# Three more pieces of a one-hot pick on ScalarE, and the expert products moved ahead of the gather

## The reference

```python
xn = batch_norm(x)                                # over all 1792 tokens
q = (xn @ w_q.T) ...                              # two halves, 8 heads
sim = einsum('pbnhd,hkpd->pbnhk', q, keys_p)      # 2 x 8 x 32 scores per token
scores, idx = top_k(sim, 8)
sc, pk = top_k(scores[0][..., :, None] + scores[1][..., None, :], 8)   # 8 of 64 pairs
indices = idx0 * 32 + idx1                        # 8 heads x 8 experts per token, of 1024
hmid = sigmoid(sc) * gelu(inputs . down[indices])
out = sum over the 64 of hmid * up[indices]
```

## Time and profile before

| | |
|---|---|
| median of 3 runs | 521.06 us (520.82 to 522.73) |
| the profiled execution | 520.97 us |
| its span, first to last instruction | 519.2 us |
| VectorE busy | 386.6 us, 74% of the span |
| TensorE busy | 442.1 us, 85% |
| ScalarE busy | 219.1 us, 42% |
| GpSimd busy | 141.5 us, 27% |
| the chain that ended last, by engine | PE 43%, DVE 43%, issue 7%, ACT 3%, DMA 1%, POOL 1% |
| its costliest VectorE lines | L880 7%, L945 6%, L884 4%, L911 3% |

### The profile page before, as it was taken

The page is one execution under the profiler, slowest core; times in us unless marked ns, Lnnn a source line. Parts: engine busy times, 40 slices in busy tenths (PEclk is TensorE's granted clock), DMA queues, the critical chain, the costliest instruction groups (busy, mean ns, idle before and its releaser), DMA issues.

```text
span 519.2 us, 14256 instructions
## 1 busy us (share of the span) xinstructions
PE 442.1 (85%) x5223; PEld 349.1 (67%) x5223; DVE 386.6 (74%) x1693; ACT 219.1 (42%) x415; POOL 141.5 (27%) x192
## 2 busy tenths in 40 slices
PE   1889999988999999999997953697978877797787
PEld 1667777764777876886785912376767676676777
DVE  2999999986554564655565579999799997999571
ACT  1554454576544453454456330425233422525240
POOL 1433333450000000000000015064463737182700
PEclk9999999999999999999999855758586775958587
DMA  8992000020066467456500000000000000000000
GB/s 227 224 210 74 0 0 0 2 82 1 8 184 166 121 163 189 122 138 188 147 3 1 1 1 1 0 4 11 4 11 4 11 1 2 11 1 11 4 11 11
DMA packets 8731, 30.51 MB, mean 59 GB/s; under 512 B 697, under 2 KB 4281, under 8 KB 8409
## 3 DMA queue, kind: packets, MB, share of 16 engines
q1 hardware_dynamic: 8680, 29.89, 22.7%
HBM read 28.97 MB, written 0.92 MB: 58 GB/s over the span
## 4 chain that ended last, share of the span: by engine, by line
PE 43%; DVE 43%; issue 7%; ACT 3%; DMA 1%; POOL 1%; DVEq 1%; SPq 0%; PEldq 0%; POOLq 0%; ACTq 0%
PE PS L1147 8%; PE PS L1165 8%; PE PS L1081 7%; DVE idx L880 7%; DVE AR L945 6%; PE PS L1155 5%; DVE val L884 4%; DVE pos L911 3%; DVE neg L720 2%; PE PS L1028 2%; PE PS L1301 2%; PE PS L994 2%; DVE best L904 2%; DVE b_hi L942 2%; DVE cand L891 2%
## 5 line engine op out<-in xcount | busy, mean ns | idle before, releaser
L1285 PE MATMUL PS<-b_hi,AR 128*128 128x16 f16 x896 | 54.6, 192 | 13.4 <-DVEq L947 13.4
L1285 PEld LDWEIGHTS PS<-b_hi,AR 128*128 128x128 f16 x896 | 53.9, 106 | 16.7 <-DVEq L947 16.7
L1286 PE MATMUL PS<-b_lo,AR 128*128 128x16 f16 x896 | 54.5, 192 | 0.0
L347 POOL TENSOR_TENSOR xn<-xn,cexp 128x1280 f16<-128x1280 f16 x14 | 33.5, 2392 | 77.1 <-DVE cand L891 68.8
L1286 PEld LDWEIGHTS PS<-b_lo,AR 128*128 128x128 f16 x896 | 54.0, 106 | 0.0
L1081 PE MATMUL PS<-KA,AR 125*128 125x125 f32 x384 | 46.8, 272 | 0.8 <-ACT AR L415 0.8
L1165 PE MATMUL PS<-AR 125*64 125x128 f32 x768 | 46.0, 277 | 0.0
L1147 PE MATMUL PS<-AR 128*64 128x500 f32 x192 | 43.8, 591 | 1.3 <-ACT XA L497 0.9
L1081 PEld LDWEIGHTS PS<-KA,AR 125*128 125x128 f32 x384 | 41.6, 141 | 4.7 <-issue 3.5
L787 DVE COPY AR<-PS 125x512 f32<-125x512 f32 x16 | 11.1, 692 | 44.8 <-PE PS L1155 44.8
L1165 PEld LDWEIGHTS PS<-AR 125*64 125x64 f32 x768 | 42.2, 138 | 2.0 <-issue 0.2
(11 more groups left out here) (146 smaller groups left out, 947.0 us busy)
## 6 DMA issues: line engine op xcount, KB each, us to landing
AR<-ctx SPq DMA_DIRECT2D x16, 1344.0 KB
AR<-ctx SPq DMA_DIRECT2D x16, 156.0 KB
KB<-pack_b SPq DMA_DIRECT2D x1, 1280.0 KB, 12.9
XA<-pack_q SPq DMA_DIRECT2D x1, 1024.0 KB, 4.8
KA<-pack_a SPq DMA_DIRECT2D x1, 965.0 KB, 6.9
XA<-x SPq DMA_DIRECT2D x4, 224.0 KB
out<-res SPq DMA_DIRECT2D x7, 128.0 KB, 1.8
XA<-zeros SPq DMA_DIRECT2D x2, 64.0 KB
```

The source lines that it names most:

```text
L347: nc.gpsimd.tensor_tensor(h4, h4, cexp[:, :, t, :].rearrange("p c (h o) -> p c h o", o=1).to_broadcast([128, NCAND, NH, TOPK]), ALU.mult). ...
L1285: mm(o, pick_u[:, n, :], b_hi[:, :, n], start=True, stop=False)
L1286: last = mm(o, pick_u[:, n, :], b_lo[:, :, n], start=False, stop=True)
```

## The change

ScalarE makes pieces 0, 13, 14 and 15 instead of piece 0 alone, and VectorE makes 1 to 12. With eu8 up to 127, piece 15 is `Relu(eu8 - 126)`, which comes out in reversed order, so the host reverses those rows of the weights `down` and `up`. Pieces 13 and 14 are `Relu(1 - Square(eu8 - 8a))`, in place, with a wait of ScalarE on itself between the two steps (`squared`). The offsets are three columns of a new tile `shift`, which GpSimd fills once. On ScalarE `gelus` and `first_u` now stand ahead of `rows` and `residual`; on TensorE `gather(i-1)` stands behind `hidden(i)` and waits for all four gelus of duo i, and round 1 of `hidden(i)` waits for the rows of i-2 instead of i-1.

```diff
+BY_ACT = (U // V - 3, U // V - 2)
...
+            for n, a in enumerate(BY_ACT):
+                ch.did(nc.gpsimd.memset(shift[:, n:n + 1], float(-a * V)))
+            ch.did(nc.gpsimd.memset(shift[:, 2:3], float(2 - U)))
...
             def first_u(i):
                 act.wait_ge(s["eu8_ready"], i + 1)
-                nc.scalar.activation(pick_u[:, :, 0:V], eu8[:, :, :], ACT.Relu, scale=-1.0, bias=1.0).then_inc(s["first_u"], 1)
+                nc.scalar.activation(pick_u[:, :, 0:V], eu8[:, :, :], ACT.Relu, scale=-1.0, bias=1.0)
+                nc.scalar.activation(pick_u[:, :, U - V:U], eu8[:, :, :], ACT.Relu, bias=shift[:, 2:3])
+                for n, a in enumerate(BY_ACT):
+                    part = pick_u[:, :, a * V:(a + 1) * V]
+                    nc.scalar.activation(part, eu8[:, :, :], ACT.Square, bias=shift[:, n:n + 1]).then_inc(s["squared"], 1)
+                    act.wait_ge(s["squared"], len(BY_ACT) * i + (n + 1))
+                    last = nc.scalar.activation(part, part, ACT.Relu, scale=-1.0, bias=1.0)
+                last.then_inc(s["first_u"], 1)
...
                     weights(i + 1, 0)
+                gelus(i)
+                first_u(i)
                 if after(i, 1):
                     rows(i - 1)
                     residual(i)
-                first_u(i)
-                gelus(i)
...
-                for a in range(1, U // V):
+                for a in range(1, BY_ACT[0]):
...
                     elif r == 1:
-                        pe.wait_ge(s["res_ready"], i + 1)
+                        if after(i, 1):
+                            pe.wait_ge(s["res_ready"], i)
...
-            def gather(i):
+            def gather(i, rounds):
                 pe.wait_ge(s["x2s_ready"], i + 1)
-                pe.wait_ge(s["h_done"], (V // 2) * (i + 1))
+                pe.wait_ge(s["h_done"], (V // 2) * rounds)
...
                 expert_transposes(i)
-                if after(i, 1):
-                    gather(i - 1)
                 if before(i, 2):
                     key_scores(i + 2, 0)
                 hidden(i)
+                if after(i, 1):
+                    gather(i - 1, i + 1)
                 spread(i, by_bank=not before(i, 1))
...
+    order = np.concatenate([np.arange(U - V), np.arange(U - 1, U - V - 1, -1)])
```

More of the change, by code:

```diff
@@ L179, in decoder_block @@
         spare = sb("spare", [128, 2])
+        shift = sb("shift", [128, 3])
         xbn = sb("xbn", [128, 2, TILE])
@@ L231, in decoder_block @@
             "xbn_ready sim_psum sim_read best_ready weight_ready index_ready hit_ready cand_ready expert_ready "
-            "x2s_ready ew_psum ew_copied ew_read eu8_ready first_u picks mix_psum bank_spread mix_copied mixed out_psum res_ready").split()}
+            "x2s_ready ew_psum ew_copied ew_read eu8_ready first_u squared picks mix_psum bank_spread mix_copied mixed out_psum res_ready").split()}
         block = stack.enter_context(nc.Block())
@@ L962, in _ @@
             with dve.Fori(0, (DUOS - 1) // 2) as i:
-                ch.enter(i, 2 * (2 * (16 + 16 + 3 + 8 + 8) + 3 + 2 + 4 + U // V - 1))
+                ch.enter(i, 2 * (2 * (16 + 16 + 3 + 8 + 8) + 3 + 2 + 4 + BY_ACT[0] - 1))
                 for j in range(2):
@@ L1323, in _ @@
             duo(DUOS - 1)
-            gather(DUOS - 1)
+            gather(DUOS - 1, DUOS)
 def constants():
@@ L1362 @@
         "keys": a["L0_ffn_keys_p"].transpose(3, 2, 0, 1).reshape(C, -1),
-        "down": a["L0_ffn_down"][:EXPERTS].reshape(U, V, C).transpose(2, 1, 0).reshape(C, -1),
-        "up": a["L0_ffn_up"][:EXPERTS].reshape(U, V * C),
+        "down": a["L0_ffn_down"][:EXPERTS].reshape(U, V, C)[order].transpose(2, 1, 0).reshape(C, -1),
+        "up": a["L0_ffn_up"][:EXPERTS].reshape(U, V, C)[order].reshape(U, V * C),
         **constants(),
```

## The result

Sixteen runs of each kernel gave 524.51 us median (522.07 to 526.97) after the change and 521.7 (520.6 to 522.73) before it: a ratio of 1.006 [1.0042, 1.0079]. The forecast was 522.5, "the same" its likeliest single case; the time came out 0.6% slower, inside the range and just past the 0.5% that the prediction counts as no change. The profiled execution took 524.71 us, its span is 522.9.

A forecast was written before the change was run, and what follows sets the result against it. VectorE was taken to set the pace in the duos; -1.5 us up to D6 (the last duo's L927 end) and +3.0 behind it gave +1.5, so 522.5 us, range 516.5 to 526.5.

The forecast's parts named there:

- the rule for M: Earliest next `ew_read` through ScalarE, spread and `mix`: 15.0 + g + f, 26.2 us at full clock, 27.9 with two half-clock rounds.
- g: Gelu block, start of hidden to end of fourth gelu: 4.6 us at full clock, 6.3 with half clock in two rounds.
- f: ScalarE's six activations for its pieces plus two waits on itself: 6.6 us, bounds 6.4 to 7.0.
- D2 to D3 and D4 to D5: Steps between duos, each dated by L927's end (`ew_read` follows): 27.05 us, the middle of two clocks, -0.1 each.
- D0 to D1: Step from duo 0 to duo 1, hidden at half clock: 27.9 us, +1.3.
- The tail: Last spread behind D6, the last duo's L927 end: 13.0 us instead of 9.99, +3.0.
- V: Step lengths if VectorE alone set them, 1.0 us less per duo: 25.6, 28.4, 26.1, 28.2, 26.1 us.
- the rival of half clock throughout: Hidden starts at half clock in every duo: D2 to D3 and D4 to D5 27.9 us, total 525.9; chance 0.27.
- Full clock in all but duo 0: Rival: hidden at full clock after duo 0, last spread 11.3 us behind D6, total 519.1 us; chance 0.15.
- The slip between the two products of `mix`: Rival: VectorE's L926 isn't held by `mix` or slips between its products; steps are V, total 517 us; chance 0.15.
- table load stands between Square and Relu: Rival: Square on ScalarE brings a 1.28 us table load into each f, +6.4, total 528.9 us; chance 0.05.
- D5 to D6: Step from duo 5 to duo 6: 26.2 us, with `mix(5)` starting at 486.15 and D6 at 491.0.

The follow-up runs named there:

- the table ahead: Changed kernel plus a one-column Gelu in front of the gelu block, loading the Gelu table before the wait for hidden: 524.04 us, ratio 1.0053.
- the products on both sides: Changed kernel, Gelu table loaded early, plus small unread TensorE products, 20 ahead of the key scores and 8 behind: 519.89 us, ratio 0.9975.
- the order alone: Changed kernel's new order on both engines, with only piece 0 on ScalarE as before: 520.91 us, ratio 1.0001.
- the filled run with the table behind the wait: Changed kernel plus 18 small unread TensorE products in front of hidden, Gelu table load left as in the change: 523.35 us, ratio 1.0026.
- table ahead, filled: Changed kernel with the Gelu table loaded early and 18 small unread TensorE products in front of hidden: 521.21 us, ratio 1.0003.
- the unfilled run with three pieces: Changed kernel with Gelu table loaded early and pieces 0, 14 and 15 on ScalarE, no small TensorE products: 519.42 us, ratio 0.9953.

## Why the prediction was right or wrong

**Right.** VectorE's pieces take 4.12 us. ScalarE takes spread's last place in every duo. The order costs nothing in the total. L938 is held by `mix` and ends with it (duo 3: 410.88 against 410.84), and the rule for M stands: with the measured g and f, 15.0 + 7.8 + 6.2 = 29.0 for D2 to D3 and D4 to D5, where 29.6 and 29.2 were measured (the 0.6 and 0.2 left over are not explained), and 27.8 for D0 to D1 (28.0). Duos 1 and 3 gained the 1.0 us, to 0.2. The tail is 2.4 us longer, forecast 3.0.

**f** was 6.6, measured 6.24, under its lower bound of 6.4: ScalarE's wait on its own semaphore takes 0.03 us (Square ends at 420.84, Relu starts at 420.87), where I took 0.2.

**The step that failed is g in D2 to D3 and D4 to D5.** Two sentences of it: that the Gelu load "falls into the wait for hidden and costs nothing", and that TensorE "may enter hidden at either clock; I take the middle, 27.05". I bounded the first properly ("without that cover it adds 1.3 to g") and then left it out of the sum. The one load in the earlier trace rows is Sigmoid's, and I carried its place over to another activation. The loads aren't in the source, so the place of each has to be read for itself: in the changed kernel Gelu's is ahead of the wait in duos 0, 5 and 6, behind it in duos 1 to 4, those of the loop. And the trace of before had Gelu's load too, among the rows that the earlier trace rows leave out, 1.2 us behind the start of hidden(3):

```profile
413.40 1.28 ACT L597 ACT_TABLE_LOAD   x1
414.70 1.08 ACT L597 ACTIVATE AR<-PS 128x512 f32 x2
```

The first two gelus run back to back behind it, and from hidden's start to the end of gelu 3 that trace took 418.07 - 412.23 = 5.8 us. My 4.6 was put together from the later rounds, and so the load fell out of it. For the second sentence, hidden ran at half clock not for two rounds, as my 6.3 had it, but for three of the four in hidden(2) and hidden(4). Together g was 7.8 where the middle of my two values is 5.45: some 1.8 us of that is the clock (7.2 with the table ahead) and 0.55 the load, and f gave 0.4 back. M passed V by 2.9 us in two steps, and these two steps missed by 4.7 us. I had the clock's part as the rival of half clock throughout, with 27.9 for these steps and 525.9 in all; its mechanism came, without the load, and its D6, 1.9 us later behind D0 than before, is close to the trace's 168.7 - 166.3 = 2.4.

**The other rivals.** Full clock in all but duo 0 did not come by itself; made by the products on both sides, it brings the spread of four pieces to 11.2 us behind D, where the rival had 11.3. The slip between the two products of `mix` happened in duo 1 (L938 takes 0.18) and was worth nothing, as L939 behind it was held for 2.33 instead; in duo 6 it was worth 2.4 us (below). No table load stands between Square and Relu. The rule that relu belongs on VectorE (the Trainium skill, ScalarE: Activation LUTs, Rules for kernel authors) holds here for the fourth piece on ScalarE, which took the ratio from 0.9953 to 1.0053. It does not hold for the second, as two pieces with the table ahead are at 0.9958 (one piece with the table ahead wasn't run), and the third neither cost nor gained anything that the times can tell.

**The sum's end, and luck.** D5 to D6 came out 1.1 us shorter than forecast although g was 6.0 in duo 5 and not 4.6. `mix(5)` started where the rule puts it, at 468.77 + 0.1 + 6.0 + 6.2 + 10.1 = 491.2 (491.39 in the trace), and its two products ended at 496.09. But L938 ended with the first of them (493.77), L939 slipped in ahead of the second, and D6 is 493.88. pick_v was held instead, for 2.62 us, and that cost nothing: VectorE's picks were done 10.8 us behind D6, ScalarE's pieces 12.3. So by this rule the slip took about 2.4 us off the time (496.09 + 0.2 against 493.88; no run was made for it). That the profiled execution came within 2.2 us of the forecast is in part luck: the two steps missed by +4.7 us, and D5 to D6 (-1.1), the tail (-0.6) and the early start of the layer (-1.0) took more than half of it back.

The start of the layer moves by itself: D0 is at 323.97 in the run of the order alone and at 327.92 in the filled run with the table behind the wait, so single executions are compared by their steps.

## What to carry to other kernels

When work is moved to an engine that was waiting, add up that engine's new chain to the point where its result is needed, at the worst clock and with every table load on the wrong side of its wait: here three pieces fitted into ScalarE's slack, and the fourth took the ratio from 0.9953 to 1.0053 (table ahead in both). A reorder that is worth nothing alone may be what makes another part of the change affordable, so undo the parts one at a time. And two losses on one chain can hide each other: the table load was worth 0.4 to 0.6 us a duo until the clock was repaired, and 1.28 after that.

## What the runs showed of the hardware

- Small products that nobody reads raised the granted clock in the hidden products behind them from 0.50 to 1.00, and 16 of these took 3.91 us (table ahead, filled) where 12 took 5.48 at 0.50 (table ahead). They are not needed every time: hidden(3) of the unfilled run with three pieces had 1.00 too. They cost nothing where TensorE was idle, and held hidden up until 0.8 to 1.3 us behind D where they ran into it.
- The exclusion between GpSimd's `mix` and VectorE works both ways: a VectorE instruction of 0.18 us took up to 2.33 beside `mix` in the changed kernel, and `mix` among VectorE's two-input picks took 7.1 us instead of 4.65.
- A Square on ScalarE beside Gelu and Relu brought no table load, in any of the runs that have one.
- Between the two products of `mix` a single VectorE instruction of 0.18 us slipped through (L938 in duo 1, L939 in duo 6), and the next one was held, for 2.33 and 2.62 us.
- ScalarE started 0.03 us behind the end of its own instruction that it waited for by a semaphore (420.84 to 420.87).
